# Moving 128 MB through one core: loads and stores of two tiles each instead of one, a cap on the first loads, and an earlier first matmul

## The reference

```python
B, C, D, T, N_SUBJECTS = (128, 128, 128, 1024, 8)
w = weights[subjects]
out = jnp.einsum('bct,bcd->bdt', x, w)
return x + out
```

## Time and profile before

| what | value |
|---|---|
| time, median of 3 runs | 325.02 us (324.95 to 325.21) |
| the profiled execution's own time | 324.97 us |
| its span | 323.2 us |
| TensorE busy | 234.3 us (72%) |
| VectorE busy | 196.0 us (61%) |
| ScalarE busy | 132.3 us (41%) |
| moved | 134.81 MB, 417 GB/s over the span |
| mean granted TensorE clock | 0.974 |

### The profile page before, as it was taken

The page is one execution under the profiler, slowest core; times in us unless marked ns, Lnnn a source line. Parts: engine busy times, 40 slices in busy tenths (PEclk is TensorE's granted clock), DMA queues, the critical chain, the costliest instruction groups (busy, mean ns, idle before and its releaser), DMA issues.

```text
span 323.2 us, 3792 instructions
## 1 busy us (share of the span) xinstructions
PE 234.3 (72%) x1024; PEld 104.4 (32%) x1024; DVE 196.0 (61%) x261; ACT 132.3 (41%) x131; POOL 0.8 (0%) x7
## 2 busy tenths in 40 slices
PE   0199999999878778777687686786776867867400
PEld 0044444444333324333333233242333332423200
DVE  3238888888855756656657557566575575663500
ACT  4026646556543433434424434334244343343400
POOL 1000000000000000000000000000000000000000
PEclk9999999999999999999999999999999999999955
DMA  7999999999999999999999999999999999999994
GB/s 288 426 421 401 422 427 431 422 426 430 425 427 429 426 426 429 427 426 428 427 427 427 427 429 427 425 432 425 427 429 426 427 429 426 426 429 427 423 430 208
DMA packets 18967, 134.81 MB, mean 417 GB/s; under 512 B 2065, under 2 KB 2578, under 8 KB 2578
## 3 DMA queue, kind: packets, MB, share of 16 engines
q1 hardware_dynamic: 9744, 67.64, 50.0%
q10 hardware_dynamic: 9218, 67.11, 49.2%
HBM read 67.63 MB, written 67.11 MB: 417 GB/s over the span
## 4 chain that ended last, share of the span: by engine, by line
DMA 64%; PE 22%; DVEq 3%; DVE 3%; issue 2%; ACT 0%; ACTq 0%; SPq 0%
DMA out<-x_ring 47%; PE product L189 22%; DMA x_ring<-x 16%; DVEq L114 2%; DMA weight_halves<-weights 1%; DVE x_ring L123 1%; DVE weight_ring L115 1%; DVE x_ring L122 0%; DVEq L40 0%; ACT weight_bank L151 0%; DVEq L115 0%; DVE weight_bank L108 0%; ACTq L163 0%; SPq L77 0%; ACTq L162 0%
## 5 line engine op out<-in xcount | busy, mean ns | idle before, releaser
L189 PE MATMUL product<-x_ring,weight_ring 64*128 64x512 f32 x1024 | 234.3, 602 | 69.1 <-DMA x_ring<-x 54.2
L189 PEld LDWEIGHTS product<-x_ring,weight_ring 64*128 64x128 f32 x1024 | 104.4, 189 | 198.1 <-issue 192.2
L122 DVE TENSOR_TENSOR x_ring<-product,x_ring 64x1024 f32<-64x1024 f32 x64 | 77.9, 1216 | 96.9 <-PE product L189 96.9
L159 ACT COPY x_ring<-product 64x1024 f32<-64x1024 f32 x64 | 64.5, 1008 | 168.8 <-PE product L189 168.8
L123 DVE TENSOR_TENSOR x_ring<-product,x_ring 64x1024 f32<-64x1024 f32 x64 | 78.5, 1227 | 0.8
L160 ACT COPY x_ring<-product 64x1024 f32<-64x1024 f32 x64 | 64.2, 1004 | 0.8
L115 DVE COPY weight_ring<-weight_bank 64x256 f32 x128 | 36.9, 288 | 7.0 <-issue 4.3
L102 DVE COPY weight_bank<-weight_halves 64x1024 f32<-64x1024 f32 x2 | 1.4, 688 | 4.7 <-DMA weight_halves<-weights 4.6
L151 ACT COPY weight_bank<-weight_halves 64x1024 f32<-64x1024 f32 x2 | 2.2, 1115 | 2.1 <-DMA weight_halves<-weights 2.1
L151 ACT ACT_TABLE_LOAD x1 | 1.3, 1283 | 1.4 <-PEq L206 1.4
L108 DVE TENSOR_TENSOR weight_bank<-weight_bank,eye 64x512 f32<-64x512 f32 x2 | 1.4, 686 | 0.3 <-ACT weight_bank L151 0.2
## 6 DMA issues: line engine op xcount, KB each, us to landing
x_ring<-x SPq DMA_DIRECT2D x64, 1024.0 KB, 12.9
out<-x_ring ACTq DMA_DIRECT2D x64, 1024.0 KB, 39.4
weight_halves<-weights SPq DMA_DIRECT2D x1, 512.0 KB, 4.0
subject_row<-subjects ACTq DMA_DIRECT2D x1, 0.5 KB
```

Source lines behind the costliest of these rows:

```text
L122: dve.tensor_tensor(x_ring[LOW, slot, 0, :], low[LOW, :], x_ring[LOW, slot, 0, :], add)
L159: act.copy(x_ring[LOW, slot, 1, :], low[HIGH, :])
L189: last = pe.matmul(product[slot % PRODUCTS][a][:, cols], weight_ring[half, slot, r, :], x_ring[half, slot, r, cols], start=r == 0, stop=r ...
```

## The change

Every load of `x` and nearly every store carries two neighbouring tiles, 2 MiB, into or out of two neighbouring slots (a place); there are 32 loads. In memory the two tiles lie 1 MiB apart from partition to partition's share: for each partition the transfer takes 8 KB of the first tile and 8 KB of the second. Semaphores of loads and stores are kept for each of the 6 places. SP issues four pair loads at first, and the fifth and sixth when the first and the second have landed. TensorE waits for a tile's load on even slots only. The four picks are still made, but TensorE starts after two. ScalarE issues a store when both tiles of a place are done; the last four tiles are stored one by one, which makes 30 + 4 = 34 stores. The waits at the end go through the places from 5 down to 0.

```diff
--- before.py
+++ after.py
@@ -6,6 +6,8 @@
 PSUM_BANK_COLS = 512
 DMA_INC = 16
 SLOTS = 12
+PAIR = 2
+LOADS_AHEAD = 4
 PICK_AHEAD = 4
 PRODUCTS = 2
 
@@ -28,14 +30,16 @@
     TILES = B // 2
     LAPS, REST = divmod(TILES, SLOTS)
     assert LAPS and SLOTS % PRODUCTS == 0 and REST % PRODUCTS == 0 and REST == PICK_AHEAD > PRODUCTS
+    PAIRS, PAIR_SLOTS = TILES // PAIR, SLOTS // PAIR
+    assert SLOTS % PAIR == 0 and REST % PAIR == 0 and LOADS_AHEAD < PAIR_SLOTS
     BANKS = T // PSUM_BANK_COLS
     LOW, HIGH = slice(0, H), slice(H, C)
     EVEN, ODD = slice(0, H), slice(H, D)
     EVENS, ODDS = slice(0, S, 2), slice(1, S, 2)
     add = mybir.AluOpType.add
 
-    x_of_tile = x.rearrange("(n a) (h r) t -> n (a h) (r t)", a=2, r=R)
-    out_of_tile = out.rearrange("(n a) (h r) t -> n (a h) (r t)", a=2, r=R)
+    x_of_pair = x.rearrange("(n j a) (h r) t -> n (a h) j (r t)", j=PAIR, a=2, r=R)
+    out_of_pair = out.rearrange("(n j a) (h r) t -> n (a h) j (r t)", j=PAIR, a=2, r=R)
 
     with ExitStack() as ctx:
         x_ring = ctx.enter_context(nc.sbuf_tensor("x_ring", [C, SLOTS, R, T], f32))
@@ -58,8 +62,9 @@
         bank_low = ctx.enter_context(nc.semaphore("bank_low"))
         eyes_added = ctx.enter_context(nc.semaphore("eyes_added"))
         bank_high = ctx.enter_context(nc.semaphore("bank_high"))
-        x_in = [ctx.enter_context(nc.semaphore(f"x_in{s}")) for s in range(SLOTS)]
-        x_out = [ctx.enter_context(nc.semaphore(f"x_out{s}")) for s in range(SLOTS)]
+
+        x_in = [ctx.enter_context(nc.semaphore(f"x_in{s}")) for s in range(PAIR_SLOTS)]
+        x_out = [ctx.enter_context(nc.semaphore(f"x_out{s}")) for s in range(PAIR_SLOTS)]
 
         picked = ctx.enter_context(nc.semaphore("picked"))
 
@@ -72,19 +77,23 @@
 
         @block.sync
         def _(sp):
-            def load(tile, slot, stored):
-                sp.wait_ge(x_out[slot], stored)
-                sp.dma_start(x_ring[:, slot, :, :], x_of_tile[bass.ds(tile, 1)]).then_inc(x_in[slot], DMA_INC)
+            def load(pair, place):
+                sp.dma_start(x_ring[:, place * PAIR:(place + 1) * PAIR, :, :],
+                             x_of_pair[bass.ds(pair, 1)]).then_inc(x_in[place], DMA_INC)
 
             sp.dma_start(weight_halves[:, :, :, :],
                          weights.rearrange("(i a) (h r) d -> (a h) i (r d)", a=2, r=R)).then_inc(weights_in, DMA_INC)
-            for slot in range(SLOTS):
-                sp.dma_start(x_ring[:, slot, :, :], x_of_tile[slot]).then_inc(x_in[slot], DMA_INC)
+            for place in range(PAIR_SLOTS):
+                if place >= LOADS_AHEAD:
+                    sp.wait_ge(x_in[place - LOADS_AHEAD], DMA_INC)
+                load(place, place)
             with sp.Fori(1, LAPS) as lap:
-                for slot in range(SLOTS):
-                    load(lap * SLOTS + slot, slot, lap * DMA_INC)
-            for slot in range(REST):
-                load(LAPS * SLOTS + slot, slot, DMA_INC * LAPS)
+                for place in range(PAIR_SLOTS):
+                    sp.wait_ge(x_out[place], lap * DMA_INC)
+                    load(lap * PAIR_SLOTS + place, place)
+            for place in range(REST // PAIR):
+                sp.wait_ge(x_out[place], LAPS * DMA_INC)
+                load(LAPS * PAIR_SLOTS + place, place)
 
         @block.gpsimd
         def _(pool):
@@ -152,15 +161,17 @@
                     weight_bank[half, subjects_of, :, :].rearrange("h i r (q k) -> h i r q k", q=2),
                     weight_halves[source, :, :, :].rearrange("h i r (k q) -> h i r q k", q=2))
 
-            def step(tile, slot):
+            def cross(tile, slot):
 
                 low, high = product[slot % PRODUCTS]
                 act.wait_ge(multiplied, tile + 1)
                 act.copy(x_ring[LOW, slot, 1, :], low[HIGH, :])
                 act.copy(x_ring[HIGH, slot, 0, :], high[LOW, :]).then_inc(copied, 1)
+
+            def whole(tile):
+
                 act.wait_ge(copied, tile + (PRODUCTS + 1))
                 act.wait_ge(summed, tile + (PRODUCTS + 1))
-                act.dma_start(out_of_tile[bass.ds(tile, 1)], x_ring[:, slot, :, :]).then_inc(x_out[slot], DMA_INC)
 
             act.dma_start(subject_row[0:1, :], subjects.rearrange("(one b) -> one b", one=1)).then_inc(subjects_in, DMA_INC)
             act.sem_inc(copied, PRODUCTS)
@@ -169,11 +180,21 @@
             bank(HIGH, HIGH, ODDS).then_inc(bank_high, 1)
             with act.Fori(0, LAPS) as lap:
                 for slot in range(SLOTS):
-                    step(lap * SLOTS + slot, slot)
+                    cross(lap * SLOTS + slot, slot)
+                    if slot % PAIR == PAIR - 1:
+                        whole(lap * SLOTS + slot)
+                        place = slot // PAIR
+                        act.dma_start(out_of_pair[bass.ds(lap * PAIR_SLOTS + place, 1)],
+                                      x_ring[:, place * PAIR:(place + 1) * PAIR, :, :]).then_inc(x_out[place], DMA_INC)
+
             for slot in range(REST):
-                step(LAPS * SLOTS + slot, slot)
-            for slot in range(SLOTS):
-                act.wait_ge(x_out[slot], DMA_INC * (LAPS + (slot < REST)))
+                place, j = divmod(slot, PAIR)
+                cross(LAPS * SLOTS + slot, slot)
+                whole(LAPS * SLOTS + slot)
+                act.dma_start(out_of_pair[LAPS * PAIR_SLOTS + place, :, j, :],
+                              x_ring[:, slot, :, :]).then_inc(x_out[place], DMA_INC)
+            for place in reversed(range(PAIR_SLOTS)):
+                act.wait_ge(x_out[place], DMA_INC * (LAPS + (PAIR if place < REST // PAIR else 0)))
 
         @block.tensor
         def _(pe):
@@ -181,7 +202,8 @@
 
                 pe.wait_ge(summed, tile + 1)
                 pe.wait_ge(copied, tile + 1)
-                pe.wait_ge(x_in[slot], landed)
+                if slot % PAIR == 0:
+                    pe.wait_ge(x_in[slot // PAIR], landed)
                 for n in range(BANKS):
                     cols = slice(n * PSUM_BANK_COLS, (n + 1) * PSUM_BANK_COLS)
                     for r in range(R):
@@ -191,7 +213,8 @@
                                              tile_position=(a * H, 0))
                 last.then_inc(multiplied, 1)
 
-            pe.wait_ge(picked, PICK_AHEAD)
+
+            pe.wait_ge(picked, PRODUCTS)
             with pe.Fori(0, LAPS) as lap:
                 for slot in range(SLOTS):
                     multiply(lap * SLOTS + slot, slot, lap * DMA_INC + DMA_INC)
```

## The result

| | before | changed |
|---|---|---|
| median of 22 runs each | 325.25 us (324.74 to 326.61) | 324.74 us (323.99 to 325.03) |
| ratio changed / before | | 0.9968 (95%: 0.9958 to 0.9979) |
| the profiled execution's own time | 324.97 us | 325.0 us |
| its span | 323.2 us | 323.2 us |

The account below looks back on a forecast made before the run. The prediction took the DMA engines' work list, ending with the slowest of 16 engines, as the bound. From 324.97 us it took 0.4 for packets and 0.1 for final waits, other terms 0 or hidden: 324.5 us, range 322.8 to 325.9.

Parts of the forecast that it names:

- Packets, 0.37 to 0.56 us: On each DMA engine, 62 fewer semaphore packets at 6 to 9 ns each save 0.37 to 0.56 us; 0.4 taken.
- First loads: At the start, four pair loads at once keep the queue filled while the fifth and sixth wait; cost 0.
- two picks: Before the first matmul, two picks instead of four start TensorE 3.0 us earlier, at 11.9; the gain is hidden.
- the end's single stores: At the end, storing the last four tiles singly brings nothing that the drain of stores does not hide.
- Pair stores: From the first store on, stores begin 0.4 us later and loads may run dry 1 or 2 us; cost 0.
- Final waits, 0.1 us: At the end, waits of 38 ns behind the last landing fall from six to one: 0.1 us gained.
- Rival 2: At the first stores, 24 to 28 us, the rate dip of 0.55 us goes: 323.9 us, chance 0.07.
- Rival 3: In pair transfers, alternating addresses 1 MiB apart slow the data packets: 326.6 us, at worst 344; chance 0.15.
- Rival 4: At about 38 us, an engine has neither loads nor stores, costing 2 us: 326.5 us, chance 0.06.
- The 124 us of the cited rule: Over all transfers, the skill's fixed cost of about 2.0 us, if unhidden, would make 62 fewer bring up to 124 us.
- the case beyond 0.2%: For the whole kernel, a gain over 0.2%, 0.65 us, counts as faster: chance 0.34, against 0.47 for the same.
- Rival 1: On the last engine, each transfer costs more than its packet, 0.05 us a tile: 1.6 us more saved, 322.9; chance 0.17.

Follow-up runs that it names:

- its two variants: Changed kernel with all six pair loads issued at first, 324.62 us (0.9966 to before); changed kernel with last four tiles stored as two pairs, 324.55 us (0.9958).
- right for four: Changed kernel with four tiles to a transfer, three loads at first, last four tiles stored singly: 340.81 us, ratio 1.0447 to the kernel before.
- that of the second: The changed kernel run again without edit, beside the kernel before on the same chip: 324.83 us, ratio 0.996 (0.9943 to 0.9977).
- five with 244: Kernel before with a 128-byte load behind each later load and each store (128 + 116 transfers): 329.14 us, ratio 1.0091.

## Why the prediction was right or wrong

- **The bound.** Right. The engines' work list sets the time, 427 GB/s before and after, and without any product the kernel is only 3.8 us faster.
- **Packets, 0.37 to 0.56 us.** Right, and seen in the changed kernel itself. The bytes of all packets that begin between 100 and 290 us give 427.3, 426.9 and 427.2 GB/s in the three profiles of the kernel before, and 427.8, 427.6, 427.6 and 427.8 in the four of the changed kernel and its two variants. That is 0.13%, 6.4 ns a tile for the one semaphore packet that a tile lost, or 0.39 us over the 294 us from 24 to 318. With pairs in the loads or in the stores alone the rate is between, 427.3 and 427.4.
- **First loads, two picks, the end's single stores.** Right, each hidden. The cap and the single stores change nothing that shows. TensorE's start was put at 11.9 and came at 12.07, the first store at 24.1 and came at 23.92. The last store was put at 10.5 us behind the last landed load and came 11.5 us behind it (302.02 to 313.57), since TensorE took 8.85 us for the last pair.
- **Pair stores.** Right: the store queue took over when the load queue ran low (40 to 48 us at 428 GB/s), and nothing went dry.
- **Final waits, 0.1 us.** Half of it came: from the last landing to the end of the span it is 0.61 us in every profile of the kernel before and 0.57 in every one of the changed kernel, so 0.04 us.
- **Rival 2.** Wrong: the dip stays. **Rival 3.** Wrong: 427 GB/s, with pairs in the loads alone too. **Rival 4.** Wrong for two tiles, right for four. Its price of 2 us from issue to first packet is not what the trace of the kernel before shows: 1.1 us for the first transfer of all (0.75 to 1.85), 3.8 us for the first store (23.69 to 27.51).
- **The 124 us of the cited rule.** The prediction takes the fixed cost of 2.0 us and the 341 and 425 GB/s from the Trainium skill (DMA: Bandwidth & Descriptors, "Anatomy of one DMA" and "Bandwidth"); both stand there for transfers that GpSimd issues, and this kernel issues none of those. The 62 transfers fewer brought 1.0 us.
- **The step that failed**, although the time came within the range, stands in the sum: 324.97 - 0.4 - 0.1, "it was 0.05 under the median, which I leave". It took the last engine's lag as a fixed thing, from one profile and three runs within 0.3 us. That lag varies in the kernel before: half of its 29 later runs are 1.0 us or more above the lowest, and the profile of one at 327.07 shows the lag two microseconds longer (5.48 us against 3.70). The changed kernel has no run above 325.03 among 34 (22 and 12). So a gain of 0.5 us became one of 0.7 to 1.4 us by the ratio of the first comparison (and up to 1.9 by that of the second), and the case beyond 0.2% came in place of "the same". That the medians differ by just the 0.5 us of the forecast is in part luck: the kernel before was at 325.02 when the forecast was made and at 325.25 in the comparison.
- **Rival 1** had the right place, "0.05 us is unexplained" on the last engine, and the wrong owner. It is not the price of a transfer as such: 128 transfers without the product leave no engine behind. The unexplained 0.05 us a tile is this engine's steady falling behind: 0.68 us in 12 tiles is 0.057 a tile. It needs compute beside it, and it seems to grow with the transfers (two microseconds alone with 128, five with 244), but one profile with 244 against a range of two to four with 128 does not show that. Pairs did not slow it either: 0.72 us in 12 tiles.

Open: what the compute engines do that slows one DMA engine, and why with fewer transfers the long executions are gone. That either half of the change removes them is shown by 12 runs of each; the mechanism is not.

## What to carry to other kernels

When the DMA engines are full from end to end, price a change in packets per engine, and look at which engine ends last and how far it is behind the others: one engine's lag on top of the mean rate makes the time. Take several runs of the kernel before ahead of a forecast of half a per cent; its spread can be larger than the gain. Here a transfer fewer was worth 6 ns as long as a backlog stood in both queues. The backlog should end up in the stores: where the tiny loads moved it into the loads, the end was bare.

## What the runs showed of the hardware that was not expected

- Transfers of 64 partitions, loads alone: 229 GB/s, against 424 for 128 partitions, the DMA engines counted as busy both times. With loads and stores together it was 423 against 427.
- 52 tiny loads in the load queue moved the backlog from the store queue (39.4 us to landing, now 12.9) into it (12.9, now 33.9); in both queues they left it in place (10.2 and 36.0). It is as if a small packet took a turn like a large one.
- One DMA engine falls behind the others steadily while compute runs, 0.6 to 1.1 us in 60, to 3.3 to 5.5 us behind the first at the end, and not at all without (0.34 us at the end, 0 GB/s from 319 to 320 us).
- The mean granted TensorE clock of the profiled execution fell from 0.974 to 0.931 in the changed kernel, and to 0.938 with pairs in the loads alone, while it was 0.990 with pairs in the stores alone. With two tiles landing together TensorE works and rests in longer turns: its longest wait for a load is 2.9 us in the changed kernel and 3.3 with pairs in the loads, against 1.4 and 1.7 with pairs in the stores. That the longer rests lower the clock is argued from these four, not shown. It costs little here, since TensorE is not the bound: the last pair's 8.85 us still ended 9.6 us before the drain.
